# GroupNorm, sign-weight 3x3 convolution and residual on one core: first and last image become units of half height, spread over both partition halves

## What is computed

```python
def reference(x, W):
    g = x.reshape(32, 32, 2, 56, 56)
    m = mean(g, axis=(2, 3, 4)); s = var(g, axis=(2, 3, 4))
    n = ((g - m) / sqrt(s + 1e-5)).reshape(x.shape)
    return x + conv3x3(n, sign(W), padding=1)
```

## Time and profile before

| | |
|---|---|
| median of 3 runs | 202.27 us (201.59 to 202.57) |
| span of the profiled execution | 200.7 us |
| median less span, taken as what lies around the span | 1.6 us |
| PE busy | 191.2 us (95%) |
| DVE, POOL, ACT busy | 165.3 (82%), 166.7 (83%), 149.7 us (75%) |
| moved by DMA | 52.17 MB, mean 260 GB/s |

### The profile page before, as it was taken

One profiled execution on the slowest core, in us unless ns is written; L12 is line 12 of the kernel. 1 busy time (PEld: TensorE's weight loads), 2 busy tenths in 40 slices (PEclk: granted clock), 3 DMA queues, 4 the chain that ended last, 5 costly groups with the idle time before them and its releaser, 6 DMA issues.

```text
span 200.7 us, 10042 instructions
## 1 busy us (share of the span) xinstructions
PE 191.2 (95%) x4482; PEld 168.4 (84%) x4482; DVE 165.3 (82%) x363; ACT 149.7 (75%) x142; POOL 166.7 (83%) x85
## 2 busy tenths in 40 slices
PE   1999999999999999999999999999999999999990
PEld 0478888879858988988999988899998999889990
DVE  2799999996999997799988779998779999627392
ACT  3185999799989289899909989972998999595000
POOL 1029786999999999999999997999999899999500
PEclk9999999999999999999999999999999999999999
DMA  6978977871787988868697887868887883906274
GB/s 216 362 217 292 331 246 252 289 209 44 306 243 291 297 316 282 282 248 278 242 301 296 275 327 276 325 228 321 326 241 296 266 319 152 381 13 238 116 283 175
DMA packets 18698, 52.17 MB, mean 260 GB/s; under 512 B 2080, under 2 KB 5024, under 8 KB 18656
## 3 DMA queue, kind: packets, MB, share of 16 engines
q1 hardware_dynamic: 18656, 51.54, 72.9%
HBM read 25.84 MB, written 25.69 MB: 257 GB/s over the span
## 4 chain that ended last, share of the span: by engine, by line
PE 65%; ACT 14%; DVE 13%; DMA 3%; issue 1%; SPq 0%; DVEq 0%; ACTq 0%
PE psum L738 65%; ACT halves L424 5%; DVE stats L500 5%; ACT xnorm L418 4%; DMA xbuf<-in_x_dram 3%; ACT moved L437 3%; DVE xbuf L570 2%; DVE xbuf L556 1%; DVE xbuf L580 1%; DVE own L508 1%; ACT line_halves L447 1%; ACT std L413 1%; DVE xbuf L544 1%; ACT lines_norm L451 1%; DVE halves L538 1%
## 5 line engine op out<-in xcount | busy, mean ns | idle before, releaser
L738 PE MATMUL psum<-halves,w_taps 64*64 64x385 f16 (+8 forms) x4140 | 183.4, 325 | 0.5 <-DVE halves L532 0.4
L738 PEld LDWEIGHTS psum<-halves,w_taps 64*64 64x64 f16 x4140 | 156.7, 107 | 19.3 <-ACT moved L437 0.9
L330 POOL TENSOR_TENSOR halves<-xnorm,halves 128x784 f16<-128x784 f32 (+5 forms) x35 | 91.6, 2637 | 20.0 <-ACT xnorm L418 19.7
L500 DVE BATCH_NORM_STATS2 stats<-xbuf 128x6 f32<-128x448 f32 x112 | 60.8, 613 | 4.3 <-DMA xbuf<-in_x_dram 4.1
L424 ACT ACTIVATE halves<-xbuf,coef 128x784 f16<-128x784 f32 (+5 forms) x35 | 50.7, 1449 | 3.0 <-DVE coef L525 2.8
L418 ACT ACTIVATE xnorm<-xbuf,coef 128x784 f32<-128x784 f32 (+5 forms) x35 | 50.5, 1443 | 0.0
L437 ACT ACTIVATE moved<-psum 64x784 f32<-64x784 f32 (+1 forms) x30 | 25.5, 850 | 7.9 <-PE psum L738 7.3
L345 POOL TENSOR_TENSOR xbuf<-xbuf,moved 128x784 f32<-128x784 f32 (+1 forms) x15 | 29.3, 1956 | 0.4 <-ACT moved L437 0.4
L570 DVE SCALAR_TENSOR_TENSOR xbuf<-psum,xbuf 64x784 f32<-64x784 f32 (+1 forms) x32 | 28.2, 881 | 1.0
L556 DVE SCALAR_TENSOR_TENSOR xbuf<-psum,xbuf 128x784 f32<-128x784 f32 x21 | 20.3, 967 | 7.6 <-PE psum L738 7.4
L371 POOL TENSOR_TENSOR line_halves<-lines_norm,line_halves 128x1512 f16<-128x1512 f32 (+1 forms) x10 | 20.9, 2120 | 0.5 <-ACT lines_norm L451 0.5
(11 more groups left out here) (36 smaller groups left out, 72.0 us busy)
## 6 DMA issues: line engine op xcount, KB each, us to landing
xbuf<-in_x_dram SPq DMA_DIRECT2D x48, 448.0 KB, 4.6
out_dram<-xbuf SPq DMA_DIRECT2D x43, 392.0 KB, 4.0
xbuf<-in_x_dram SPq DMA_DIRECT2D x16, 224.0 KB, 4.1
out_dram<-xbuf SPq DMA_DIRECT2D x5, 504.0 KB, 3.9
out_dram<-xbuf SPq DMA_DIRECT2D x5, 448.0 KB, 3.8
out_dram<-xbuf SPq DMA_DIRECT2D x5, 364.0 KB, 4.1
out_dram<-xbuf SPq DMA_DIRECT2D x5, 252.0 KB, 4.1
out_dram<-xbuf SPq DMA_DIRECT2D x1, 224.0 KB, 3.8
```

The source lines that it names most:

```text
L330: nc.gpsimd.tensor_tensor(at(halves[:, k % HRING, 1, :], a, b), at(xnorm[:, k % NRING, :], a, b), at(halves[:, k % HRING, 0, :], a, b), AL ...
L500: nc.vector.bn_stats(stats[:, n, :], xbuf[:, s, n * STAT:(n + 1) * STAT]).then_inc(blocks_ready, 1)
L738: mm = pe.matmul(outs[:, :, left:right], weights, ins[:, :, left + dx:right + dx], start=first_step, stop=last_step)
```

## The change

Image 0 and image 31 are taken out of the pairs and become units 0 and 16 of half height: rows 0 to 27 lie in LOW, rows 28 to 55 in HIGH, each with a row of the other half beside it (30 rows in `xbuf`, of which one is an edge of zeros). Fifteen whole pairs lie between, so there are 17 units. Five of them still use lines, now 4, 7, 10, 12 and 14. The statistics of a half unit are four `bn_stats` of 7 rows and two copies that carry each half's figures to the other. The first chunk's lo goes from DVE to POOL. The HIGH halves and the weights are loaded on ACT's DMA queue, the LOW halves on SP's, each in two pieces; the last image is stored on both queues. PE's fillers no longer wait for the first piece (13 rounds, then 5 after the turn). The third coefficient is made for line pairs only.

```diff
-WARM_UP = 17
-KEEP_WARM = 4
-WINOGRAD = (3, 6, 9, 12, 14)
+WARM_UP = 13
+KEEP_WARM = 5
+WINOGRAD = (4, 7, 10, 12, 14)
...
-    NP = B // 2
+    NP = B // 2 + 1
     LAST = NP - 1
+    SPLIT = (0, LAST)
+    HALF = H // 2
...
     def home_units(k):
+        if k == 0:
+            return [[(1, 7), (15, 7)]]
         if k == LAST:
-            return [[(0, 7), (14, 7)], [(28, 7), (42, 4)], [(50, 3)]]
+            return [[(1, 7)], [(15, 4)], [(23, 3)]]
...
     def away_units(k):
+        if k == 0:
+            return [[(8, 7), (22, 7)]]
         if k == LAST:
-            return [[(7, 7), (21, 7)], [(35, 7), (46, 4)], [(53, 3)]]
+            return [[(8, 7)], [(19, 4)], [(26, 3)]]
...
+    HALVES = [(0, 15), (15, HALF + 2)]
+    LAST_ROWS = [(1, 14), (15, 8), (23, 6)]
...
         @block.sync
-            for n in range(NPIECE):
-                start_load(sp, 0, n)
-            sp.dma_start(w_raw[:], w.rearrange("o c h w -> o (c h w)")).then_inc(w_loaded, 16)
+            for n in range(len(HALVES)):
+                start_half_load(sp, 0, LOW, n)
             for n in range(NPIECE):
                 start_load(sp, 1, n)
...
+            store_unit(LAST - 1, 1)
+            for n, (first, rows) in enumerate(LAST_ROWS):
+                sp.wait_ge(home_done, home_before(LAST) + 1 + n)
+                wait_away(LAST, n)
+                half_store(sp, LAST, LOW, n, first, first + rows)
...
         @block.scalar
+            for n in range(len(HALVES)):
+                start_half_load(act, 0, HIGH, n)
+            act.dma_start(w_raw[:], w.rearrange("o c h w -> o (c h w)")).then_inc(w_loaded, 16)
...
+            for n, (first, rows) in enumerate(LAST_ROWS):
+                act.wait_ge(home_done, home_before(LAST) + 1 + n)
+                act.wait_ge(away_done, 2 * aways_before(away_before(LAST) + n + 1))
+                half_store(act, LAST, HIGH, n, first, first + rows)
...
         @block.vector
+            def split_stats(k):
+                here = split_before(k)
+                for n in range(4):
+                    if n % 2 == 0:
+                        dve.wait_ge(top_loaded[n // 2], 16 * (here + 1))
+                        dve.wait_ge(bottom_loaded[n // 2], 16 * (here + 1))
+                    nc.vector.bn_stats(stats[:, n, :],
+                                       at(xbuf[:, k % XRING, :], 1 + BR * n, 1 + BR * n + BR)).then_inc(blocks_ready, 1)
+                dve.wait_ge(blocks_ready, stats_before(k + 1))
+                for ours, theirs in ((LOW, HIGH), (HIGH, LOW)):
+                    nc.vector.tensor_copy(stats[ours, 4:8, :], stats[theirs, 0:4, :]).then_inc(crossed, 1)
+                dve.wait_ge(crossed, 2 * (here + 1))
...
         @block.tensor
-            pe.wait_ge(loaded[0][0], 16)
             pe.wait_ge(filler_ready, 1)
             warm(WARM_UP)
...
-                        r0, r1 = max(b.first, -dy), min(b.first + b.rows, H - dy)
+                        top, bottom = data_rows(b.pair, lanes)
+                        r0, r1 = max(b.first, top - dy), min(b.first + b.rows, bottom - dy)
```

More of the change, by code:

```diff
@@ L125, in aways_before @@
     def aways_before(u):
-        return sum(0 if by_scalar(k, i) else len(away_units(k)[i]) if k == LAST and i else 1 for k, i in AWAY[:u])
+        return u - moves_before(u)
     def winograd_before(k):
@@ L149, in conv_preact_kernel, with first_row, image_rows, whole_before @@
     NPIECE = len(PIECES)
+    HALVES = [(0, 15), (15, HALF + 2)]
+    LAST_ROWS = [(1, 14), (15, 8), (23, 6)]
+    def first_row(k):
+        return 1 if k in SPLIT else 0
+    def image_rows(here, a, b):
+        if here == LOW:
+            return max(a, 1) - 1, b - 1
+        return HALF - 1 + a, min(HALF - 1 + b, H)
+    def whole_before(k):
+        return sum(j not in SPLIT and j % XRING == k % XRING for j in range(k))
+    def split_before(k):
+        return sum(j in SPLIT for j in range(k))
+    def stats_of(k):
+        return 4 if k in SPLIT else NSTAT
+    def stats_before(k):
+        return sum(stats_of(j) for j in range(k))
     with ExitStack() as ctx:
@@ new lines, in _ @@
+                    sp.wait_ge(away_conv, away_blocks_before(k) + 2)
+                    if new == LAST:
+                        load_half(new, LOW, 1)
+                        load_half(new, HIGH, 1)
+                    else:
+                        load(new, 2)
+                        load(new, 3)
+                if k == 0:
+                    sp.wait_ge(home_done, 1)
+                    wait_away(0, 0)
+                    store_half(0, LOW, 0, 1, HALF + 1)
+                    store_half(0, HIGH, 0, 1, HALF + 1)
+                    continue
@@ L570, in add_away @@
                     nc.vector.scalar_tensor_tensor(part[here], made[there], 1.0 / SCALE,
-                                                   part[here], ALU.mult, ALU.add).then_inc(away_done, 1)
-            def add_last(n, home, away):
-                dve.wait_ge(home_conv, home_blocks_before(LAST, 1) + n + 1)
-                add_rows(LAST, home.bank, home.first, home.rows).then_inc(home_done, 1)
-                dve.wait_ge(away_conv, away_blocks_before(LAST, 1) + n + 1)
-                part = at(xbuf[:, LAST % XRING, :], away.first, away.first + away.rows)
-                for here, there in ((LOW, HIGH), (HIGH, LOW)):
-                    nc.vector.scalar_tensor_tensor(part[here], psum[there, away.bank, 0:away.rows * W], 1.0 / SCALE,
                                                    part[here], ALU.mult, ALU.add).then_inc(away_done, 1)
@@ L681, in last_chunk, with data_rows @@
                 k = b.pair
-                return next(n for n, (a, z) in enumerate(chunks(k)) if min(b.first + b.rows, H - 1) < z)
+                last_row = HALF + 1 if k in SPLIT else H - 1
+                return next(n for n, (a, z) in enumerate(chunks(k)) if min(b.first + b.rows, last_row) < z)
+            def data_rows(k, lanes):
+                if k not in SPLIT:
+                    return 0, H
+                return (1, HALF + 2) if lanes == LOW else (0, HALF + 1)
             def wait_upper(b):
```

170 lines of the change are left out of this document (110 added, 60 removed).

## The result

The change made the kernel slower: 216.45 us (215.97 to 217.02) against 202.0, a ratio of 1.071 with a 95% interval of 1.068 to 1.074. The forecast was 202.1, the range 200.8 to 203.9. The profiled execution took 215.97 us, its span 214.2; that of before was 200.7.

The account below looks back on a forecast made before the run. PE was taken to run full from 12.35 to 195.89 us. Head -2.67, waits +2.9, edges +0.2, stall -0.54 and tail 0 summed to -0.1 after rounding: 202.1 us, no change, range 200.8 to 203.9.

Parts of the forecast that it names:

- DVE's two copies for the last image and twelve third coefficients ... cancel under PE: Middle of the kernel: added copies and dropped coefficients (0.13 us each) on DVE cancel, at no cost to PE.
- The head, 2.67 us earlier: Start: second pieces land at 5.4 us, so PE's first convolution step comes at 9.68 instead of 12.35.
- my first rival: Start and last store: short transfers land sooner, second pieces at 4.6 us; time 201.0 us; chance 0.27.
- the rival of half the rate: End units' loads and stores: 64 partitions move at half the rate; 203.6 us, or 204.6 at 210 KB/us; chance 0.20.
- The weights: Start: third on ACT's queue, landing at 5.0 to 8.1 us; PE starts at 11.4 at worst, 1.7 late, free.
- The wait ahead of unit 1: After unit 0: PE waits 1.55 us for ACT's hi and 1.35 for POOL's lo, giving back the head's gain.
- Unit 0 may finish 2.9 us late at no cost: Start: the waits ahead of unit 1 cover PE and ACT delays in unit 0, up to 2.9 us.
- The 0.54 behind the first line pair: Middle: PE's 0.54 us stall after the first line pair, which came from ACT, is gone (bounds 0 and 0.54).
- GpSimd, 1.0 us spare in unit 14: Late middle: POOL loses 1.24 us in a second tight turn, leaving 1.0 of 2.2 us spare, no cost.
- The clock rival: Start: PE's clock falls in the waits and unit 1 runs 5 us at 1.2 GHz; 204.6 us; chance 0.09.
- The tail: End, behind PE's last product: last store on two queues changes nothing, 0 us (bounds 0.3 less, 0.8 more).

Follow-up runs that it names:

- x1: Changed kernel with the two small copies between partition halves written as VectorE's 32-lane shuffle: 206.91 us, ratio 1.025.
- x9: Kernel before with fifteen probe rounds ahead of its work, small VectorE operations issued while GpSimd runs back to back; its time is of no interest.
- x3: Changed kernel with GpSimd waiting, before its work for the last image, until VectorE's two copies are done: 208.14 us, ratio 1.029.
- x8: x4 with the weights' load also held until the first image's four half-partition pieces have landed: 208.67 us, one execution.
- x6: x4 with 18 rounds of TensorE warm-up instead of 13: 206.19 us, ratio 1.019.
- x5: x1 with 24 rounds of TensorE warm-up instead of 13: 206.55 us, ratio 1.018.
- x4: x1 with pair 1's loads held until the first image's four half-partition pieces have landed: 206.47 us, ratio 1.022.

## Why the prediction was wrong

**The step that failed** is "DVE's two copies for the last image and twelve third coefficients ... cancel under PE", with the copies priced at 0.13 to 0.21 us each. I took the price from the nearest rows, a small constant operation and a shuffle. The shuffle is a form that x1 and x9 show is not held. The constant operation has one number per partition, and fifteen like it took 0.20 us each beside GpSimd in before, while x9's of 24 numbers was held for 1.08. For the first image, with GpSimd idle, the price was right (0.17). For the last it was 11.07, to the end of GpSimd's work from 172.02 to 184.29; that it is held beside GpSimd is shown by x1, x3 and x9, why it missed four ends stays open. I had read that GpSimd's row was full there and used it only for GpSimd's own lateness. It is worth 6.7 us of waiting and 3.2 of half clock, where the sum had nothing; x1 gives 9.5 of the 14.4 us back.

The Trainium skill, "SBUF — State Buffer", section "Who interferes with whom", has the rule: VectorE and GpSimd share a pair of ports as an exclusive lock; copies and operations with constants can need it, and an operation with both inputs in SBUF needs part of it beside a GpSimd instruction that reads SBUF. x9 agrees, with 1.08 us for each such form beside a GpSimd instruction of 1.67, and 0.17 for the shuffle. I had not cited this rule, and it was the one that spoke against the change. It says that the later one waits for the whole instruction of the other; 36 held operations agree, and five, up to 11.07 us over several instructions, do not.

**The head, 2.67 us earlier**, was right in kind and wrong in size. The second pieces came at 6.98 in after and as late as 8.55 with the same loads, 6.5 to 6.7 with a hold, not at 5.4: my first rival, at 4.6, was furthest off, and the rival of half the rate came true in its first part ("it decides once the second pieces land after 5.7"), not in its last store. x8 moved 208 to 239 GB/s from 3.5 us on, where before moved 373 to 416. In x6, with the clock mended, the first step is 1.15 us earlier instead of 2.67. The estimate from the Trainium skill in the prediction, 6.7 for the landing, was nearer than my 5.4. With the halves alone, two queues gained next to nothing over one (6.54 and 6.61).

**The weights**, "there at 5.0 to 8.1", were a term with bounds too narrow: they landed at 8.90 in after, 6.74 us after their issue, and x5's took 8.0. They, and not the first upper half, set the first step at 12.31.

**The wait ahead of unit 1**, 1.55 and 1.35, was right: x6 shows 1.39 and 1.15. In after the first part is hidden, because unit 0 starts late and runs at half clock until 13.6 us.

**"Unit 0 may finish 2.9 us late at no cost"** was wrong. When it does, VectorE's add of unit 0 moves back, the statistics of unit 2 behind it start at 22.19 in after (20.50 in x6), and TensorE waits 0.31 us for VectorE's add at 33.12 (0.71 in x1, nothing in x6). The 0.54 behind the first line pair did go: from 34.90 to 170.34 TensorE did not stop.

**GpSimd, 1.0 us spare in unit 14**, was too much: a wait of 0.36 stands at 172.18 in after, and about that in x1 and x3.

**The clock rival** (0.09) came true in the part that I had not priced: the pause of 3.26 us ahead of the weights, not the wait for unit 1, took the clock to the lower level, and so did the 6.71 us. "TensorE: Matmul & The Clock Gate" of the Trainium skill, section "HAM oscillation — how this bites in real kernels", warns of idle gaps between bursts, and the rows at 10 to 14 and 184 to 192 us agree. In x6, with pauses of 0.26 and 1.12 us, the clock stayed at 1.00.

**The tail** was right: 0.2 us more in after, 0.1 less in x1.

With the copy mended, the versions of the changed kernel stand at 1.018 to 1.029 (x1, x3 to x6): slower, as the last two rivals had it, and in part for their reasons, the late pieces and the clock, but by more than their 203.6 to 204.6. What x6 still has over before, pauses and longer work of the start, is read from its profile and not taken apart by a run. No term of the sum had an upper bound that reached 216. Two slips of the working change nothing: by its own terms the two waits are 1.53 and 1.41, not 1.55 and 1.35, and 448 KB from 4.19 to 5.6 us are 318 KB per us, not 310.

## What to carry to other kernels

Before a small VectorE operation is put on a critical order, look at which form it has and what GpSimd does at that moment: a duration from a stretch where GpSimd is idle says nothing for one where it is full. Price a new operation by what is queued behind it for as long as GpSimd's longest run, and take a form that is not held (here the shuffle). A transfer into half of the partitions is no half transfer: 812 KB in such pieces were there at 6.54 us at the earliest, 896 KB in whole ones by 5.6.

## What was not expected of the hardware

- A copy of 64 x 24 numbers that took 0.17 us with GpSimd idle took 11.07 beside it, past four ends of its instructions; in 36 other cases held operations got in at the first end, and a shuffle of the same numbers was never held (0.17 to 0.18).
- TensorE's pause of 1.70 us in x4, after 4.84 us of fillers, was followed by 0.50 of granted clock until 16 us; those of 1.12 and 1.39 us in x6, after longer work, by 1.00. No run separates the pause from the work ahead of it.
- Half-partition loads kept the transfer engines busy (a share of 0.91 to 1.05 from 3.5 to 5.0 us) while they moved 208 to 276 GB/s, against before's 373 to 416, on one queue as on two.
- The same half-partition loads, with the same transfers beside them, were there between 6.98 and 8.55 us in six profiles.
